# Order of the expert rounds, their waits and their loads in a fused Mamba, experts, attention and fp4 kernel

## The reference, cut to what matters

```python
x = x + mamba(ln(x))      # a scan over the tokens, 256 channels x 16 states
x = x + experts(ln(x))    # 8 experts, top 2, one after the other (below)
x = x + attention(ln(x))  # 6 layers, 16 heads of 8, double softmax, feed-forward
x = x + fp4_ffn(ln(x))

# experts, for each token:
vals, idx = top_k(softmax(x @ gate_W + gate_b), 2)
e0 = expert(idx[0], x)                    # relu(x @ W1 + b1) @ W2 + b2
e1 = expert(idx[1], x + 0.5 * e0)         # needs the first expert's result
out = layernorm(x + vals[0] * e0 + vals[1] * e1)
```

## Time and profile before

| what | value |
|---|---|
| median of 3 runs | 2826.67 us (2818.91 to 2829.14) |
| the profiled execution | 2813.64 us, span 2811.8 us |
| busy: VectorE, TensorE, ScalarE, GpSimd | 2458.1, 2392.2, 2302.9, 1433.5 us |
| first 46 us | loads and first chunk's preparation |
| 46 to 355 us | the scan |
| 355 to 386 us | round 0 |
| 390 to 433 us | round 1 (its last scatter begins at 432.66) |
| 425 to 470 us | round 2 |
| 501 to 530 us | round 3 |
| 531 to some 2700 us | the attention |
| 2700 to 2811.8 us | the end of the fp4 layer |

### The profile page before, as it was taken

How to read it: one execution, slowest core, us unless ns; L and a number is a source line. 1 busy time by engine, 2 the same in 40 slices (tenths; PEclk the granted TensorE clock), 3 DMA queues, 4 the chain that set the end, 5 groups by cost and what they waited for, 6 DMA issues and landing times.

```text
span 2811.8 us, 93918 instructions
## 1 busy us (share of the span) xinstructions
PE 2392.2 (85%) x38335; PEld 1274.7 (45%) x38335; DVE 2458.1 (87%) x3438; ACT 2302.9 (82%) x4212; POOL 1433.5 (51%) x2865
## 2 busy tenths in 40 slices
PE   6778684788998998999889989899999998999856
PEld 3444473434444444444444444445444444444435
DVE  4988943699999999999999899999999999999956
ACT  5877632579998998999999899999999999999832
POOL 3443454235644665456644566445664456643564
PEclk8988887689999999999999999999999999999978
DMA  4000023413122131221222121221212212120000
GB/s 134 1 1 1 23 77 87 82 32 61 23 44 47 31 53 30 47 41 36 44 39 47 34 44 31 52 47 32 45 31 52 47 33 45 31 36 11 2 1 16
DMA packets 75119, 110.44 MB, mean 39 GB/s; under 512 B 7425, under 2 KB 69761, under 8 KB 72129
## 3 DMA queue, kind: packets, MB, share of 16 engines
q1 hardware_dynamic: 72256, 99.35, 18.5%
q0 software_dynamic: 2432, 5.08, 0.6%
HBM read 79.41 MB, written 29.05 MB: 39 GB/s over the span
## 4 chain that ended last, share of the span: by engine, by line
PE 38%; issue 18%; ACT 11%; DVE 11%; POOL 9%; DMA 1%; DVEq 0%; SPq 0%; ACTq 0%; POOLq 0%
PE bank L767 12%; PE bank L698 12%; PE bank L778 10%; ACT E L1038 9%; DVE NM L1409 7%; ACT acc L989 1%; POOL acc L1626 1%; POOL H L1636 1%; PE bank L679 1%; POOL H L1639 1%; POOL smp L1619 1%; DMA UNITB<-second 1%; PE bank L692 1%; POOL dg L1684 1%; ACT UB L1000 1%
## 5 line engine op out<-in xcount | busy, mean ns | idle before, releaser
L1409 DVE TENSOR_REDUCE NM<-bank 128x1 f32<-128x1024 f32 x1536 | 1800.2, 1208 | 82.4 <-PE bank L767 62.3
L1038 ACT ACTIVATE E<-bank,NM 128x1024 f32<-128x1024 f32 x1536 | 1707.5, 1118 | 189.0 <-DVE NM L1409 139.5
L767 PE MATMUL bank<-KS,QS 72*32 72x512 bf16 x12288 | 975.1, 390 | 163.5 <-ACT E L1038 113.7
L778 PE MATMUL bank<-E,dg 128*32 128x256 f32 x12288 | 941.2, 387 | 6.0 <-issue 4.2
L1684 POOL TENSOR_TENSOR dg<-mask,RZ 128x128 f32<-128x128 f32 x384 | 153.0, 398 | 863.7 <-DVE RZ L1419 758.4
L767 PEld LDWEIGHTS bank<-KS,QS 72*32 72x32 bf16 x12288 | 260.9, 96 | 706.3 <-ACT E L1038 583.2
L778 PEld LDWEIGHTS bank<-E,dg 128*32 128x32 f32 x12288 | 393.6, 112 | 297.0 <-issue 71.3
L1038 ACT ACTIVATION_READ_ACCUMULATOR E<-bank,NM 128x1 f32 x1536 | 310.6, 202 | 0.0
L1626 POOL TENSOR_TENSOR acc<-acc,rel 128x256 f32<-128x256 f32 x384 | 272.3, 729 | 7.8 <-ACT acc L989 7.8
L698 PE MATMUL bank<-H,ET 128*32 128x129 f32 x6144 | 194.9, 277 | 13.7 <-issue 7.3
L698 PEld LDWEIGHTS bank<-H,ET 128*32 128x32 f32 x6144 | 175.4, 111 | 41.5 <-issue 18.7
(11 more groups left out here) (262 smaller groups left out, 2651.7 us busy)
## 6 DMA issues: line engine op xcount, KB each, us to landing
KS<-scratch SPq DMA_DIRECT2D x72, 384.0 KB
QS<-scratch SPq DMA_DIRECT2D x216, 128.0 KB
scratch<-UB SPq DMA_DIRECT2D x144, 128.0 KB
WL<-in_wl SPq DMA_DIRECT2D x6, 1091.0 KB, 12.1
first<-in_fill SPq DMA_DIRECT2D x2, 990.0 KB, 8.2
second<-in_fill SPq DMA_DIRECT2D x2, 990.0 KB, 10.2
WAX<-first SPq DMA_DIRECT2D x2, 528.0 KB, 4.8
UNITB<-second SPq DMA_DIRECT2D x2, 528.0 KB, 13.5
```

The lines of the kernel that those rows point to most:

```text
L767: inst = PE_.matmul(bank[x % 3][32 * i:32 * i + 32, k * 512:k * 512 + 512], QS[0:72, half % 2, 4 * hq + i, r0:r0 + 32], KS[0:72, b, 4 * hq ...
L778: inst = PE_.matmul(pb(6)[32 * k:32 * k + 32, 256 * grp:256 * grp + 256], dg[:, x // 4 % 3, x % 4, :], E[:, x % NE, :].rearrange("p (i k c ...
L1038: A_.activation(E[:, x % NE, :], bank[x % 3][:, :], ACT.Exp, bias=NM[:, x % 4:x % 4 + 1], accum_out=ZS[:, quad % 3, j:j + 1]).then_inc(s[" ...
L1409: V.tensor_reduce(NM[:, x % 4:x % 4 + 1], bank[x % 3][:, :], AX.X, ALU.max, negate=True).then_inc(s["rowmax"], 1)
```

## The change

- **Waits.** The expert numbers are read into registers ahead of the round, at the steps in `KNOWN`, and VectorE picks a unit's weights one step earlier (`weights_dve`, for `rounds(p + 1)`). The norms n00, n01 and n02 move from VectorE to GpSimd (a new branch `n0` in `expert_pool`). The last chunk's `outp` and `x1` come at offsets 9 and 10 instead of 16 and 17 (`LASTLY`), and so do bn03, n03, the gates and G00 to G30 of the second batch, which now lie in round 0 and in front of round 1; `mask0` and the `bet` pieces move forward too.
- **rank** works on bf16 copies of its 0 and 1 matrices, 9 matmuls in place of 16.
- **First results first.** `in1` moves on GpSimd from step 154, inside round 1, to step 168, behind round 1's last scatter.
- **Order.** f, the norms and the first half's projection stand at steps 169 to 176, in front of round 2, which begins at 178 instead of 167; round 3 begins at 196. The second half's projection lies in round 2 (179 to 184).
- **Loads.** The rows of rounds 1, 2 and 3 are issued by ScalarE at the round's first step and no longer by SyncE. `KS` is laid out so that a half's 16 heads are contiguous on a partition (16 KB rows in place of 16 pieces of 1 KB).

```diff
@@ -32,29 +32,33 @@
                  30: "ut0 ut1"},
          "DVE": {-4: "bn", -3: "var", 0: "xn", 18: "rest", 20: "low", 22: "one", 25: "sum"},
          "POOL": {-3: "pow", 0: "xa", 3: "res", 26: "u0", 27: "u1"}}
-DONE = {"PE": {16: "outp"}, "ACT": {}, "DVE": {4: "y2", 17: "x1"}, "POOL": {5: "yz0", 6: "yz1"}}
-
-GATES = {"PE": {87: "etr0", 88: "etr1", 90: "gate0", 91: "gate1", 106: "rank0", 119: "etr2", 121: "gate2", 148: "etr3", 149: "gate3", 152: "rank1"},
-         "ACT": {88: "etr0", 89: "etr1", 96: "exp0", 120: "etr2", 148: "etr3", 149: "exp1"},
+DONE = {"PE": {14: "outp"}, "ACT": {}, "DVE": {4: "y2", 14: "x1"}, "POOL": {5: "yz0", 6: "yz1"}}
+
+LASTLY = {"PE": {9: "outp"}, "ACT": {}, "DVE": {4: "y2", 10: "x1"}, "POOL": {5: "yz0", 6: "yz1"}}
+
+GATES = {"PE": {87: "etr0", 88: "etr1", 90: "gate0", 91: "gate1", 106: "rank0", 119: "etr2", 121: "gate2", 142: "etr3", 143: "gate3", 150: "rank1"},
+         "ACT": {88: "etr0", 89: "etr1", 96: "exp0", 120: "etr2", 142: "etr3", 144: "exp1"},
          "DVE": {94: "g00", 97: "g02", 98: "g04", 99: "g06", 101: "g08", 102: "g10", 103: "g12", 104: "g14", 105: "g16", 106: "g18",
                  108: "g19", 109: "g21", 111: "g23", 112: "g25", 113: "g27", 114: "g29",
-                 150: "G02 G03 G04", 151: "G10 G11", 152: "G16 G17", 153: "G21 G22", 154: "G27"},
-         "DVE2": {79: "tok0", 80: "bn00", 81: "bn01", 83: "n00", 85: "n01", 92: "gl0", 93: "gl1", 94: "g01", 97: "g03", 98: "g05",
+                 145: "G02 G03", 146: "G06 G07", 147: "G10 G11", 148: "G14 G15", 149: "G18"},
+         "DVE2": {79: "tok0", 80: "bn00", 81: "bn01", 92: "gl0", 93: "gl1", 94: "g01", 97: "g03", 98: "g05",
                   99: "g07", 101: "g09", 102: "g11", 103: "g13", 104: "g15", 105: "g17", 108: "g20", 109: "g22", 111: "g24",
-                  112: "g26", 113: "g28", 114: "g30", 115: "bn02", 117: "n02", 123: "gl2",
-                  146: "bn03", 147: "n03", 149: "gl3", 150: "G05 G06 G07", 151: "G12 G13", 152: "G18", 153: "G23 G24",
-                  154: "G28 G29 G30", 170: "f0", 171: "f1", 173: "n10", 174: "bn20", 175: "n11", 176: "bn21", 177: "n20", 178: "n21"},
-         "DVE3": {149: "G00 G01", 150: "G08 G09", 151: "G14 G15", 152: "G19 G20", 153: "G25 G26", 170: "bn10", 171: "bn11"},
-         "POOL": {81: "pow00", 82: "pow01", 115: "in0", 116: "pow02", 147: "pow03", 150: "mask0 bet0", 151: "bet1", 154: "in1", 167: "bet2", 168: "bet3",
-                  171: "pow10", 172: "pow11", 174: "pow20", 176: "pow21"}}
-
-PROJECT = {"PE": {179: ((-4, "pjt"),), 180: ((-4, "pjq00"), (-4, "pjq01")), 181: ((-4, "pjq10"), (-4, "pjq11")),
-                  183: ((-3, "pjt"),), 184: ((-3, "pjq00"), (-3, "pjq01")), 185: ((-3, "pjq10"), (-3, "pjq11"))},
-           "ACT": {179: ((-4, "pjc"),), 180: ((-4, "pjo0"),), 181: ((-4, "pjo1"),), 182: ((-4, "part0"),), 183: ((-3, "pjc"), (-4, "part2")),
-                   184: ((-3, "pjo0"),), 185: ((-3, "pjo1"),), 186: ((-3, "part0"),), 187: ((-3, "part2"),)},
-           "DVE": {182: ((-4, "part1"),), 183: ((-4, "part3"),), 186: ((-3, "part1"),), 187: ((-3, "part3"),)}}
-
-ROUND = (133, 150, 167, 184)
+                  112: "g26", 113: "g28", 114: "g30", 115: "bn02", 123: "gl2",
+                  139: "bn03", 141: "n03", 143: "gl3", 145: "G04", 146: "G08", 147: "G12", 148: "G16",
+                  150: "G19 G20 G21 G22 G23 G24 G25 G26 G27 G28 G29 G30",
+                  169: "f0", 170: "f1", 171: "n10", 172: "bn20 n11", 173: "bn21", 174: "n20", 175: "n21"},
+         "DVE3": {143: "G00 G01", 145: "G05", 146: "G09", 147: "G13", 148: "G17", 169: "bn10", 170: "bn11"},
+         "POOL": {81: "pow00", 82: "n00", 83: "pow01", 84: "n01", 91: "bet0", 95: "bet1", 115: "in0", 116: "pow02", 117: "n02", 123: "bet2", 139: "mask0",
+                  140: "pow03", 142: "bet3", 168: "in1", 169: "pow10", 170: "pow11", 172: "pow20", 173: "pow21"}}
+
+PROJECT = {"PE": {174: ((-4, "pjt"),), 175: ((-4, "pjq00"), (-4, "pjq01")), 176: ((-4, "pjq10"), (-4, "pjq11"), (-3, "pjt")),
+                  179: ((-3, "pjq00"), (-3, "pjq01")), 182: ((-3, "pjq10"), (-3, "pjq11"))},
+           "ACT": {174: ((-4, "pjc"),), 175: ((-4, "pjo0"),), 176: ((-4, "pjo1"), (-4, "part0"), (-4, "part2"), (-3, "pjc")),
+                   180: ((-3, "pjo0"),), 182: ((-3, "pjo1"), (-3, "part0")), 184: ((-3, "part2"),)},
+           "DVE": {176: ((-4, "part1"), (-4, "part3")), 182: ((-3, "part1"),), 184: ((-3, "part3"),)}}
+
+ROUND = (133, 151, 178, 196)
+KNOWN = {"PE": {122: 0, 149: 1, 169: 2, 195: 3}, "DVE": {120: 0, 126: 1, 167: 2, 194: 3}}
 UNITS, WIDE = 15, 132
 ROWS = UNITS * 128
 ENDED = ROUND[3] + UNITS + 2
...
@@ -64,7 +68,8 @@
 
     out = []
     for k in range(CHUNKS):
-        out += [(k, x) for x in DONE[engine].get(p - 32 * (k + 1), "").split()]
+        done = DONE if k < CHUNKS - 1 else LASTLY
+        out += [(k, x) for x in done[engine].get(p - 32 * (k + 1), "").split()]
         if k:
             out += [(k, x) for x in READY[engine].get(p - 32 * (k - 1), "").split()]
     return out
...
@@ -364,7 +369,7 @@
 
         pk, pn, pm = ExitStack(), ExitStack(), ExitStack()
         QS = sbuf(pk, "QS", [128, 2, NHEAD, 512], BF16)
-        KS = sbuf(pk, "KS", [128, 2, NHEAD, L], BF16)
+        KS = sbuf(pk, "KS", [128, 2, 2, NHEAD, 512], BF16)
         H = sbuf(pn, "H", [128, 3, RT, 129])
         WL0 = sbuf(pn, "WL0", [128, WCOLS])
         UB = sbuf(pn, "UB", [128, 2560])
...
@@ -618,9 +625,9 @@
                 for j, x in gates("PE", p):
                     expert_pe(e, j, x)
                 for r, u in rounds(p):
-                    if u == 0:
-                        chosen = experts_of(e, mybir.EngineType.PE, r)
-                    unit_pe(e, r, u, chosen)
+                    unit_pe(e, r, u, chosen[r])
+                if p in KNOWN["PE"]:
+                    chosen[KNOWN["PE"][p]] = experts_of(e, mybir.EngineType.PE, KNOWN["PE"][p])
                 for n, x in PROJECT["PE"].get(p, ()):
                     post_pe(e, n, x)
 
...
@@ -655,11 +662,10 @@
                 inst.then_inc(s["gate"], 1)
             else:
                 e.wait_ge(s["oh"], j + 1)
-                PE_.matmul(o[:, 0:128], mc_("below"), OH[:, batch(j), :].rearrange("p t c -> p (t c)"), start=True, stop=False)
+                PE_.matmul(o[:, 0:128], below[:, :], OH[:, batch(j), :].rearrange("p t c -> p (t c)"), start=True, stop=False)
+                PE_.matmul(o[:, 128:144], ones[:, :], OH[:, 8 * j + 7, :], start=False, stop=False)
                 for t in range(7):
-                    PE_.matmul(o[:, 16 * t + 16:128], mc_("ones"), OH[:, 8 * j + t, :].unsqueeze(1).to_broadcast([128, 7 - t, 16]), start=False, stop=(t == 6))
-                for t in range(8):
-                    inst = PE_.matmul(o[:, 128:144], mc_("ones"), OH[:, 8 * j + t, :], start=(t == 0), stop=(t == 7))
+                    inst = PE_.matmul(o[:, 16 * t + 16:144], ones[:, :], OH[:, 8 * j + t, :].unsqueeze(1).to_broadcast([128, 8 - t, 16]), start=False, stop=(t == 6))
                 inst.then_inc(s["rank"], 1)
 
         def unit_pe(e, r, u, chosen):
...
@@ -941,6 +947,8 @@
                 for j, x in gates("ACT", p):
                     expert_act(e, j, x)
                 for r, u in rounds(p):
+                    if r and u == 0:
+                        rows_of(e, r)
                     unit_act(e, r, u)
                 for n, x in PROJECT["ACT"].get(p, ()):
                     post_act(e, n, x)
...
@@ -1165,6 +1174,9 @@
                         e.wait_ge(s["carry"], carried(p - 32))
                     V.tensor_tensor_scan(hs[:, p % NH, :], dA[:, p % 4, :], pb(4 + p % 2), carry[:, u:u + 1] if k % 2 else 0.0,
                                          ALU.mult, ALU.add).then_inc(s["scan"], 1)
+                for r, u in rounds(p + 1):
+                    if u < UNITS:
+                        weights_dve(e, UNITS * r + u, chosen[r][u])
                 for j, x in gates("DVE", p):
                     expert_dve(e, own, j, x)
                 if 0 <= p - 1 < CSTEPS:
...
@@ -1174,13 +1186,13 @@
                 for j, x in gates("DVE2", p):
                     expert_dve(e, own, j, x)
                 for r, u in rounds(p):
-                    if u == 0:
-                        chosen = experts_of(e, mybir.EngineType.DVE, r)
-                    unit_dve(e, own, r, u, chosen)
+                    unit_dve(e, own, r, u)
                 for j, x in gates("DVE3", p):
                     expert_dve(e, own, j, x)
                 for n, x in PROJECT["DVE"].get(p, ()):
                     post_dve(e, n, x)
+                if p in KNOWN["DVE"]:
+                    chosen[KNOWN["DVE"][p]] = experts_of(e, mybir.EngineType.DVE, KNOWN["DVE"][p])
 
         def fence_dve(e, k):
             V.memset(tiny[0:1, 4:5], 0.0).then_inc(s["fence_dve"], 1)
...
@@ -1554,6 +1568,10 @@
                 k = int(p[3])
                 e.wait_ge(s["ebn"], 9 * NORM[k, j] + 9)
```

(22 more changed lines are left out.)

36 lines of the change are left out of this document (15 added, 21 removed).

## The result

Twenty executions of each kernel, in turn on one chip: before 2824.91 us median (2817.42 to 2832.52), after 2804.4 us (2788.32 to 2819.14); ratio 0.993, 95% interval 0.9914 to 0.9946. That is 20.5 us faster, beyond the 0.5%; the forecast was 2802. The profiled execution took 2800.23 us, its span is 2798.4 us.

What follows compares the result with a forecast made beforehand. VectorE bounds the attention; between scan and attention (355 to 531 us) no engine does. Attention at 506.0 instead of 530.8 gives -24.8 us, from the 2826.67 median 2801.9, forecast 2802; own range 2794 to 2810, whole range 2786 to 2819.

Steps and rivals of the forecast that it cites:

- Scan and round 0: Scan about 1 us shorter (from -5 to +3); round 0's last scatter at 380.5 us in place of 385.6 (378 to 385).
- Gap before round 1: Last scatter to first transpose stays 4.2 us; register loads, rank and G19 to G30 counted hidden, uncovered they cost 5.
- B: Rival, 10%: register loads uncovered in the scan, rank and G30 hold up round 1 by 5 us; gain 15.4, 2811 us.
- Round 1: 3 us to the third transpose, then 21.7 without `in1` among the scatters: last scatter at 409.4, not 432.7 us.
- In front of round 2: pow10 waits for `in1` until 420.5; norms and the first half's projection leave TensorE mostly idle; first transpose at 444.5 us.
- Round 2: 27 us including the second half's projection; last scatter at 471.5 against 469.18 us, all earlier gains spent.
- the 2 us for units that fall out of step: In round 2, ScalarE and VectorE fall out of step with TensorE at part0 and part2: 2 us (0 to 4).
- In front of round 3: Rows come from ScalarE's queue, not behind SyncE's: 8.5 us in place of 32.2, first transpose at 480 (475.7 to 493).
- Round 3: 28 us less 3 us of projection, taken as 24.5; last scatter at 504.5, attention at 506.0 in place of 530.8 us.
- the window: Idle 32 us before round 3, 469 to 501 us, its rows issued behind K and Q; 8 us should replace it.
- rival A: 11%: transfers stay the bound, round 3's rows take 21 us from the other queue too; gain 9, 2817.4 us.
- Rival D: 5%, with any other loss: slower `KS` rows of 16 KB make the attention wait at changes of unit; 2841 us and more.

Runs made afterwards that it cites:

- rest_alone: Changed kernel, but SyncE again issues the rows of rounds 1 to 3, round 3's between the first half's Q and the second half's stores: 2798.87 us, ratio 0.9949.
- plain_round1: Changed kernel with round 1's 15 scatters replaced by plain writes from SyncE, so mixed lacks the reference's order; executed once: 2786.95 us.
- order_alone: Kernel before, but SyncE issues round 3's rows ahead of the first half's stores, K and Q, in the same queue: 2817.4 us, ratio 0.9959.
- queue_alone: Kernel before, but ScalarE instead of SyncE issues the rows of rounds 1 to 3, at the round's first step: 2802.93 us, ratio 0.9919.
- regs_at_use: Changed kernel, but experts' numbers are loaded into registers at the round's first use, as in the kernel before: 2805.84 us, ratio 0.9921.
- after_again: Changed kernel, unchanged, timed and profiled once more beside the kernel before: 2805.12 us, ratio 0.9930.
- plain_round1b: Changed kernel with round 1's 15 scatters as plain SyncE writes, profiled a second time on another occasion; executed once: 2797.65 us.
- weights_at_p: Changed kernel, but VectorE's copy of an expert's weights is back at the unit's own step; register loads stay early: 2809.24 us, ratio 0.9932.

## Why the prediction was right, point by point

The changed kernel itself has no calm trace. Two calm traces of its variants stand beside the first, disturbed one: rest_alone, whose rows come from SyncE, and from round 2 on plain_round1, which has the changed kernel's queues but no scatters in round 1.

| us | forecast | after | rest_alone | plain_round1 |
|---|---|---|---|---|
| last scatter of round 0 | 380.5 | 385.93 | 380.64 | 386.18 |
| first transpose of round 1 | 384.7 | 390.22 | 384.78 | 390.37 |
| last scatter of round 1 | 409.4 | 418.16 | 408.96 | none |
| first transpose of round 2 | 444.5 | 451.51 | 450.94 | 443.70 |
| last scatter of round 2 | 471.5 | 483.32 | 481.84 | 472.20 |
| first transpose of round 3 | 480 | 494.23 | 487.34 | 482.18 |
| last scatter of round 3 | 504.5 | 522.81 | 511.24 | 509.75 |
| first scores | 506.0 | 524.23 | 512.68 | 511.21 |

- **Scan and round 0.** 380.5 was met in one calm trace and missed by 5.7 us in the other. The last scan instruction begins anywhere from 345.8 to 351.4 us in the 14 traces (four of the old scan 345.8 to 350.7, ten of the new 346.7 to 351.4), which no term foresaw; the 1 us that the scan was to give is not to be seen in that.
- **Gap before round 1.** 4.2 us was forecast, and 385.93 to 390.22 is 4.3: the register loads, rank and G19 to G30 were hidden, B's waits didn't come. ScalarE's four issues took 1.91 us, close to SyncE's, as taken.
- **Round 1.** 24.7 us was forecast from first transpose to last scatter; 24.2 in the calm trace, 27.9 in the disturbed one. With `in1` inside, as before, it took 42.9 and 42.1 us on calm occasions and 48.8 and 48.9 on a disturbed one (order_alone, queue_alone): moving `in1` also took 8 scatters away from the units, a gain that no term foresaw.
- **In front of round 2.** pow10 begins at 429.24, at the end of `in1`, as said; from then to the first transpose it took 22.3 us, where 24.0 was forecast (420.5 to 444.5). That rest_alone is late here isn't the change's: SyncE issues the mixed rows there behind its wait for `first`, at 423.28, and n1 begins 13 us behind the end of `in1` (433.34) and not 1.
- **Round 2.** Forecast 27, measured 31.8, 30.9 in rest_alone and 28.5 in plain_round1. A term of this sum was too small: against the 2 us for units that fall out of step, 2.9 were spent on the first unit alone in rest_alone, transposed at 450.94 and copied at 453.86, since ScalarE does part2 and the second half's copy first. rest_alone is 3.9 us over the forecast without pauses, so they are the smaller part of the 4.8.
- **In front of round 3.** Forecast 8.5, measured 10.9. The forecast took 4.2 for an empty queue and 4.3 for what is in flight, and looked only at K and Q of the first half, gone by 482. What I left out was the K load of the second half, which SyncE issued at 483.51. Six traces have it, each with the landing of the last scatter and then the load:

  | | K issued behind the scatter's start | landing | load | scatter to transpose |
  |---|---|---|---|---|
  | after | 0.2 | 8.57 | 2.94 | 10.9 |
  | regs_at_use | 0.2 | 7.61 | 2.98 | 9.9 |
  | after_again | 0.8 | 4.28 | 6.80 | 11.2 |
  | plain_round1b | 0.9 | 2.62 | 8.34 | 11.0 |
  | weights_at_p | 2.7 | 3.16 | 9.71 | 10.6 |
  | plain_round1 | 4.4 | 4.58 | 10.25 | 10.0 |

  K on the way goes with about the same total everywhere; only whether the scatter or the load shows it changes. In rest_alone nothing was issued there, the landing took 3.66 and the load 2.27, and the transpose came after 5.5 us.
- **Round 3.** Forecast 24.5; 23.9 in rest_alone, 28.6 in the first trace with its pauses, and 27.6 in plain_round1 though it is calm: the second part of its rows landed only for a transpose at 487.48, 5.3 us behind the first, with the K load beside it.
- **Sum.** Forecast 24.8. The medians say 20.5. Calm traces of before start the scores at 530.79 and 534.46, the two calm variants at 511.21 and 512.68, 18 to 23 us earlier; neither variant is the change itself, and rest_alone's median moved by 12.6 only. The errors in round 2 (1.5 to 4.8 us) and in front of round 3 (1.4 to 2.7 in the six traces) both point the same way. In the first trace the terms miss by 5.4 up to the end of round 0, 0.1, 3.2, -1.8, 4.8, 2.4 and 4.1: together 18.2 us, 524.23 in place of 506.0.
- **What was luck.** 18.2 us late in its own trace and yet 2.4 us off in the median: the forecast took a gain reckoned on a calm trace and carried 13 us over to the median of disturbed executions without a reason. That fits only if both kernels lose about the same when disturbed, before 14 by its medians and after, as an estimate from one trace, 18.2 less the 4.3 by which the forecast gain was too large, 13.9. Nothing in the prediction foresaw it. The slips in its arithmetic are small: the projection's terms add to 11.0 and not 11.3, round 3's 28 less 3 is 25 and not 24.5, the scan's -1.6 and 1 are -0.6.
- **Where the gain comes from.** By the prediction's own sum the new order is spent when round 2 ends (471.5 against 469.18) and the window gives it all. queue_alone, 0.9919, bears that out: on top of the queue the order adds nothing that these intervals show.
- **The reason given for the window.** That SyncE issues the rows behind K and Q was right. That ScalarE's queue mends it was right too, but it isn't needed: with Q issued 25 us ahead, SyncE's queue does as well. And where K or Q had only just been issued, rival A came in by half: 8.34 to 10.42 us of 21.11.
- **Rival D.** From the attention's start to the span's end it took 2274.8 to 2283.6 us in the four traces with the old `KS` and 2271.5 to 2282.2 in the ten with the new one. No loss is to be seen; an isolated test of the layout wasn't made, but queue_alone has the old one and gains as much as the whole.

The Trainium skill, "DMA: Bandwidth & Descriptors", section "Queues, rings and completion order", says that a DMA engine takes turns between queues and that a completion waits for that engine's earlier writes in all its queues. The traces agree: rows on a queue of their own take 2.94 to 10.42 us with K or Q in flight, not 21.11, and a scatter on GpSimd's queue lands in 2.29 us alone and in 8.57 and 11.48 beside SyncE's loads.
